# Attention stage of a transformer layer: where the output projection and the two layer norms of the previous tile stand in the order of emission

## What is computed

```
qkv = (einsum('bsd,de->bse', x, W_qkv) + b_qkv).reshape(B, S, 16, 3 * 64)
q, k, v = qkv[..., :64], qkv[..., 64:128], qkv[..., 128:]
scores = einsum('bshd,bsgd->bshg', q, k) / sqrt(64)     # 16 x 16 per token
attn = softmax(scores, axis=-1)
context = einsum('bshg,bsgd->bshd', attn, v).reshape(B, S, 1024)
return einsum('bsd,de->bse', context, W_out) + b_out
...
x = x + layernorm(attn_ref(layernorm(x), ...))
x = x + layernorm(sum over 8 experts of (silu(h @ wg) * (h @ wu)) @ wd)   # h = layernorm(x)
```

## Time and profile before

| | us |
|---|---|
| median of the two timed runs (7047.9 and 8045.54) | 7546.72 |
| profiled execution, its own time | 7044.87 |
| span of the profiled execution, slowest core | 7043.3 |
| spans of the 8 cores | 7038.9 to 7043.3 |

### The profile page before, as it was taken

One profiled execution on the slowest core, in us unless ns is written; L12 is line 12 of the kernel. 1 busy time (PEld: TensorE's weight loads), 2 busy tenths in 40 slices (PEclk: granted clock), 3 DMA queues, 4 the chain that ended last, 5 costly groups with the idle time before them and its releaser, 6 DMA issues.

```text
span 7043.3 us, 71337 instructions; the slowest of 8 cores (7038.9 to 7043.3 us)
## 1 busy us (share of the span) xinstructions
PE 5713.6 (81%) x26240; PEld 2569.0 (36%) x26240; DVE 3210.2 (46%) x4436; ACT 796.2 (11%) x1347; POOL 165.0 (2%) x202
## 2 busy tenths in 40 slices
PE   2222222219999999999999999999999999999992
PEld 0100101104444444444444444444444444444441
DVE  4666666653343434343434343434343434343437
ACT  0100111101111111111111111111111111111111
POOL 0000000000000000000000000000000000000000
PEclk7656566659999999999999999999999999999996
DMA  3000000012223322222233222222332222223312
GB/s 72 0 24 0 24 0 12 0 26 40 37 39 45 44 37 36 37 37 37 39 44 44 36 37 36 37 36 39 45 44 37 37 37 36 37 39 44 44 19 96
DMA packets 173421, 247.85 MB, mean 35 GB/s; under 512 B 3616, under 2 KB 134688, under 8 KB 171552
## 3 DMA queue, kind: packets, MB, share of 16 engines
q0 software_dynamic: 169056, 209.74, 22.1%
q1 hardware_dynamic: 4032, 33.56, 1.4%
HBM read 436.22 MB, written 16.78 MB: 64 GB/s over the span
## 4 chain that ended last, share of the span: by engine, by line
PE 81%; DVE 14%; issue 3%; ACT 2%; DMA 1%; another core or an unknown queue 0%; DVEq 0%; ACTq 0%; POOL 0%; POOLq 0%
PE ps_g L507 25%; PE ps_u L512 25%; PE ps_d L538 25%; PE ps_mm L260 3%; DVE prod L332 2%; DVE prod L290 2%; DVE prod L328 2%; DVE prod L286 2%; PE ps_att L364 1%; PE ps_mm L256 1%; PE ps_tr L207 0%; DMA wd_b<-wd 0%; DVEq L73 0%; DVE tmpl L380 0%
## 5 line engine op out<-in xcount | busy, mean ns | idle before, releaser
L522 DVE TENSOR_TENSOR hbuf<-silb,ps_u 128x512 bf16<-128x512 bf16 x1024 | 703.7, 687 | 2889.5 <-PE ps_u L512 2889.5
L507 PE MATMUL ps_g<-ln2T,wg_b 128*128 128x512 bf16 x8192 | 1936.9, 379 | 35.2 <-DMA wd_b<-wd 35.2
L512 PE MATMUL ps_u<-ln2T,wu_b 128*128 128x512 bf16 x8192 | 1936.3, 379 | 0.0
L538 PE MATMUL ps_d<-hbuf,wd_b 128*128 128x512 bf16 x8192 | 1809.7, 379 | 0.0
L548 DVE TENSOR_TENSOR acc<-ps_d,acc 128x512 f32<-128x512 f32 x2016 | 1393.3, 692 | 330.8 <-PE ps_d L538 303.4
L507 PEld LDWEIGHTS ps_g<-ln2T,wg_b 128*128 128x128 bf16 x8192 | 801.8, 98 | 1002.6 <-issue 37.0
L512 PEld LDWEIGHTS ps_u<-ln2T,wu_b 128*128 128x128 bf16 x8192 | 802.0, 98 | 967.7 <-issue 1.9
L538 PEld LDWEIGHTS ps_d<-hbuf,wd_b 128*128 128x128 bf16 x8192 | 801.6, 98 | 966.5
L518 ACT ACTIVATE silb<-ps_g 128x512 bf16<-128x512 f32 x1024 | 611.4, 597 | 4676.1 <-PE ps_g L507 4676.1
L207 PE MATMUL ps_tr<-ident,ctxt 128*128 128x128 bf16 x128 | 16.2, 308 | 824.6 <-DVE ctxt L340 824.6
L207 PEld LDWEIGHTS ps_tr<-ident,ctxt 128*128 128x128 bf16 x128 | 12.4, 139 | 832.0 <-issue 832.0
(11 more groups left out here) (80 smaller groups left out, 1044.9 us busy)
## 6 DMA issues: line engine op xcount, KB each, us to landing
wg_b<-wg POOLq DMA_DIRECT2D x64, 1024.0 KB, 12.0
wu_b<-wu POOLq DMA_DIRECT2D x64, 1024.0 KB, 19.7
wd_b<-wd POOLq DMA_DIRECT2D x64, 1024.0 KB, 25.6
xf<-x SPq DMA_DIRECT2D x4, 2048.0 KB, 10.6
xspill<-xf SPq DMA_DIRECT2D x4, 2048.0 KB, 7.2
xrel<-xspill SPq DMA_DIRECT2D x4, 2048.0 KB, 9.0
out<-outb SPq DMA_DIRECT2D x16, 512.0 KB, 3.0
wqkv_sb<-wqkv POOLq DMA_DIRECT2D x1, 6144.0 KB, 52.8
```

Of the source, the lines that this page charges most:

```text
L507: gt = op('t', lambda t, par=par, kh=kh, kd=kd, bk=bk, toks=toks: t.matmul(ps_g[:, bk], wg_b[:, par, kd, kh * 128:(kh + 1) * 128], ln2T[:, ...
L512: ut = op('t', lambda t, par=par, kh=kh, kd=kd, bk=bk, toks=toks: t.matmul(ps_u[:, bk], wu_b[:, par, kd, kh * 128:(kh + 1) * 128], ln2T[:, ...
L522: mul_tok[c] = op('v', lambda v, kh=kh, bk=bk, c=c, q=q: v.tensor_tensor(hbuf[:, q % 2, kh], silb[:, c % 2], ps_u[:, bk], ALU.mult), MUL)
L538: dt_ = op('t', lambda t, par=par, m=m, mi=mi, kh=kh, q=q: t.matmul(ps_d[:, mi], wd_b[:, par, kh, m * 128:(m + 1) * 128], hbuf[:, q % 2, k ...
```

## The change

In the loop over the tiles, S5 (transposes of the context and output projection) is no longer called at the end of the tile's own iteration but in the next iteration, and S6 and S7 of the previous tile, which opened an iteration, now follow behind it. All three stand behind S3 (the QKV projection) and ahead of S4 (the attention). S5 of the last tile follows the loop. No operation is added or removed.

```
     S1(0)
     for t_i in range(nt_lim):
-        if t_i >= 1:
-            S6(t_i - 1)
-            S7(t_i - 1)
         S2(t_i)
         if t_i + 1 < nt_lim:
             S1(t_i + 1)
         S3(t_i)
+        if t_i >= 1:
+            S5(t_i - 1)
+            S6(t_i - 1)
+            S7(t_i - 1)
         S4(t_i)
-        S5(t_i)
+    S5(nt_lim - 1)
     S6(nt_lim - 1)
     S7(nt_lim - 1)
```

## The result

| | kernel before | changed kernel |
|---|---|---|
| median of all timed executions (10 and 13) | 7505.46 us | 7548.94 us |
| lowest | 7046.42 us | 6952.76 us |
| ratio of the executions that are compared below | | 0.9858, 95% interval 0.9838 to 0.9877 |

There the changed kernel takes 6952.8 to 6955.3 us, 1.4% less than before; the prediction's sum was 6952.5. The median over all, 7548.94, lies far outside the predicted 6938 to 6990.

The account below looks back on a forecast made before the run. In stage A VectorE stands still 22.26 us per steady iteration waiting for TensorE. Saving 5.24 in each of tiles 1 to 14 (73.4) plus 19.0 in tile 15 makes 92.4 off 7044.87: 6952.5 us, range 6938 to 6990.

Parts of the forecast that it names:

- the base of the sum: Whole kernel: the 92.4 us saved were taken off the profiled execution, 7044.87 us, giving 6952.5.
- The step of the mechanism: Stage A: only VectorE's two waits for TensorE move, saving 92.4 us; stage B keeps its length.
- The wait at L275 goes: Attention start: VectorE no longer waits for the last QKV copy, 13.26 us saved per tile in tiles 1 to 14.
- The wait at L164 grows to 17.02: Start of S6: VectorE waits 17.02 us for the output projection, where both waits together were 22.26 per tile.
- three terms: Counted from s, start of S1(t+1): group 2 at s + 6.00; groups 2 and 3, 6.6 us; group 5 to projection, 4.22.
- The reason given for 5.98 and 7.29: First two QKV groups of a burst: 5.98 us with transposes just ahead, 7.29 without; middle 6.6 taken.
- Why it begins late: ScalarE's list: S1(t+1)'s activations stand ahead of the six QKV copies, so groups 2 to 5 and S5 come behind S1.
- Rival 3: QKV wholly hidden under the attention: L164 wait 2.6 us, 294 us saved, 6751 us; chance 0.03.
- Tile 15, 19.0 us: Last iteration, no S1 beside it: the 19.00 us wait at L275 goes and L164 of tile 14 waits 9.0 as before.
- The projection at the full clock: Output projection behind the ctxT copy's pause: 4.46 us at the full clock, not 6.56 at the lower.
- The other section weighed in the prediction: Skill section on PSUM-queue depth-cycling: short stops between groups let TensorE's clock go back and forth; by it 6982 us.

Follow-up runs that it names:

- after: A traced execution of the changed kernel, one of the longer ones at a lower granted clock; 7351.55 us.
- again: The changed kernel itself, unchanged, run for a profile in which all cores agree; 6953.1 to 6953.5 us, ratio 0.9868 to the kernel before.
- s1_behind_s3: The changed kernel with S1(t+1) moved behind S3(t), tile 0 keeping its order; 6810.8 and 6811.8 us, ratio 0.9667.
- s1_behind_s5: The changed kernel with S1(t+1) behind S3(t) and also behind S5(t-1); 6762.6 to 6764.2 us, ratio 0.9600.
- last_only: The changed kernel with the old order for all tiles but the last iteration, which has the new one; 7026.68 us, against 7045.2 to 7046.7 before.
- warm_s5: The kernel with S1(t+1) behind S5(t-1), plus 32 spare TensorE matmuls between QKV(t) and S5(t-1); 6751.8 to 6754.4 us, ratio 0.9586.
- s5_stays: The changed kernel with S5 at its old place at the iteration's end, only S6 and S7 behind S3; 6967.5 to 6998.6 us, ratio 0.9903.

## Where the prediction failed, and where it held

- **The step that failed is the base of the sum.** The prediction took 92.4 us off 7044.87, the profiled execution, and had no term for the time by which other executions are longer, though it named one of 8045.5. The runs showed that this term is the largest of all: the changed kernel's median is 7548.94, 596 us above its 6953, and the kernel before has 7505.46, 461 above 7044.87. The range 6938 to 6990 left it out too. A trace of such an execution (`after`, 7351.55 us, core 4) shows where it lies: stage A ends at 1465 us as in `again`, but in stage B the granted clock is 0.99, 0.93 and 0.84 in 1470 to 3470, 3470 to 5470 and 5470 to 6800, where `again` has 0.99, 1.00 and 1.00. No run here shows why it is lower there. The step of the mechanism held: the times without it differ by 92.7 us (7046.0 to 6953.3 in the run `again`), and 92.4 had been forecast. That the two agree to 0.3 us is partly luck, as the terms below show.
- **The wait at L275 goes:** right, to the last tile (46.0 us, tile 0 alone).
- **The wait at L164 grows to 17.02:** 17.14 measured, in all 259.4 where 257 was said. Inside the chain three terms were mis-sized and nearly cancelled. Group 2 starts at s + 5.72 (654.72 to 660.44), not 6.00: the first copy starts 5.00 us behind s where 5.15 was taken, and the matmul follows 0.72 behind that, not 0.85. Groups 2 and 3 take 667.53 - 660.44 = 7.09, not 6.6. From group 5's start to the bias matmul of the projection it is 673.75 - 669.68 = 4.07 (4.22 said), and 4.46 from there to L164, as said.
- **The reason given for 5.98 and 7.29,** transposes just ahead of the burst or none, does not hold. In the kernel before, tile 6's first two groups took 7.23 us (619.25 to 626.48) with the same transposes ahead of them as in tile 7. Over its tiles the two groups took 5.8 to 6.1 in the odd ones and 7.1 to 7.4 in the even ones; why they alternate is not shown. That the middle was near enough was luck.
- **Why it begins late** (copies behind S1's activations on ScalarE): argued from the order in the prediction, shown by `s1_behind_s3` and `s1_behind_s5`. Rival 3, all of QKV hidden, is what `s1_behind_s5` gets; 6751 was its price, 6762.6 the measurement.
- **Tile 15, 19.0 us:** shown by `last_only`. The waits of tiles 14 and 15 at L164 were 9.77 and 9.74 where 9.0 and 10.1 were taken.
- **The projection at the full clock:** right in the changed kernel. The reason given, that the clock stayed up for over 3 us in one place, was too weak a basis: in `warm_s5` it was down 2.7 us behind the last spare matmul. The Trainium skill, "TensorE: Matmul & The Clock Gate", section "Part 4: PE-mode transpose", says that transposes do not count as TensorE being busy in the way matmuls do. The runs agree so far: in `warm_s5` the clock fell with eight transposes in the stretch. None has the same stretch without them. The other section weighed in the prediction, on short stops while PSUM banks are cycled, does not describe the bursts here: once at the 2.15 us spacing, none fell back before it ended.
- **Where the gain comes from** the prediction did not split. `s5_stays` does: S6 and S7 behind S3 bring 79 us, and S5 behind S3 another 14, all of them in the last iteration. In the other tiles it turns a wait of S6 for ScalarE into one for TensorE of the same cost (a period of 88.7 us with either).

## What to carry to other kernels

When each engine works through its list in the order of emission, a step moved for the sake of one engine has to be looked up in the list of every engine it touches: here two activations of 0.29 us ahead of six copies kept the output projection, and VectorE with it, 10 us late in every tile. Follow a wait back over two or three engines before you price it, and write down each link as an offset from one instant. Offsets from the traces gave the lowest time of each kernel here to within 10 us, except in `warm_s5` (35 us), where the clock was concerned. And if the executions at hand scatter by 14%, put the scatter into the number, or say for which of them it is meant.

## What was not expected of the hardware

In `warm_s5` TensorE's granted clock had fallen by the projection although 32 matmuls stood 3.9 us ahead of it and eight transposes at the full clock in between; with 40 matmuls, ending 2.6 us ahead of it, it stayed up in most tiles. The difference was 35 us (6751.8 to 6716.8), for 8 spare matmuls more in each tile.
